# Latent attention with a linear layer, one core: PV and out-projection of the first chunk in other units, and a chunk's input loaded from ScalarE

## The reference

```python
q = (x @ wq.T).reshape(B, S, N_HEADS, QK_HEAD)          # 16 heads, 128 + 64 values
q_pe = apply_rope(q_pe, cos, sin); k_pe likewise        # the 64 rotary values
q_lat = jnp.einsum('bshd,hdc->bshc', q_nope, wkv_b_h[:, :NOPE])
kv_cache = rmsnorm(kv_lat, kv_norm_w)                   # 128 values a token, for all heads
scores = (jnp.einsum('bshc,btc->bsht', q_lat, kv_cache) + jnp.einsum('bshr,btr->bsht', q_pe, k_pe)) * SCALE
attn = jax.nn.softmax(jnp.where(causal[None, :, None, :], scores, NEG_INF), axis=-1)
out_lat = jnp.einsum('bsht,btc->bshc', attn, kv_cache)
out = jnp.einsum('bshc,hdc->bshd', out_lat, wkv_b_h[:, NOPE:])
return out.reshape(B, S, N_HEADS * VDIM) @ wo.T
```

## Time and profile before

| | us |
|---|---|
| median of three runs (lowest, highest) | 1892.62 (1886.29, 1893.92) |
| the profiled execution | 1894.48 |
| its span, first to last instruction | 1892.0 |
| lies around the span | 2.5 |
| mean granted TensorE clock | 0.969 of full speed |

### The profile page before, as it was taken

One profiled execution on the slowest core, in us unless ns is written; L12 is line 12 of the kernel. 1 busy time (PEld: TensorE's weight loads), 2 busy tenths in 40 slices (PEclk: granted clock), 3 DMA queues, 4 the chain that ended last, 5 costly groups with the idle time before them and its releaser, 6 DMA issues.

```text
span 1892.0 us, 28195 instructions
## 1 busy us (share of the span) xinstructions
PE 1717.4 (91%) x9326; PEld 1452.8 (77%) x9326; DVE 1211.1 (64%) x2801; ACT 850.7 (45%) x1358; POOL 1008.2 (53%) x635
## 2 busy tenths in 40 slices
PE   6988788878899999799999999979999999999996
PEld 5877666656778877578888888868888888888875
DVE  4674466655666677466776776657666666666663
ACT  4554334433344454345445445434544544454442
POOL 4674444442365556355655655635555565664654
PEclk9898899988999999899999999989999999999998
DMA  6995355563756656656555554555665564655543
GB/s 201 362 329 198 102 151 146 158 190 101 201 148 174 170 156 163 182 150 179 158 149 145 158 149 135 162 166 143 175 162 130 150 162 119 166 143 130 148 121 105
DMA packets 127184, 309.12 MB, mean 163 GB/s; under 512 B 29442, under 2 KB 41987, under 8 KB 125508
## 3 DMA queue, kind: packets, MB, share of 16 engines
q1 hardware_dynamic: 98720, 233.33, 43.1%
q10 hardware_dynamic: 28324, 74.05, 15.0%
HBM read 113.28 MB, written 34.60 MB: 78 GB/s over the span
## 4 chain that ended last, share of the span: by engine, by line
PE 62%; issue 11%; DVE 7%; POOL 4%; ACT 3%; DMA 1%; SPq 1%; ACTq 1%; POOLq 0%; DVEq 0%
PE p_score L1106 25%; PE p_out L1126 18%; PE p_result L1138 7%; PE p_lat L1086 7%; PE p_rot L1086 5%; POOL pT L1389 2%; DVE acc L1241 2%; DVE turned L1200 2%; ACT qp_h L1328 1%; DVE rot_sin L1216 1%; DVE probs L1178 1%; SPq L991 1%; POOL qp_l L1378 1%; POOL qp_l L1381 1%; PE p_score L1110 1%
## 5 line engine op out<-in xcount | busy, mean ns | idle before, releaser
L1389 POOL TENSOR_TENSOR pT<-pT,pT_h 128x1024 fp32r<-128x1024 f32 x320 | 688.6, 2178 | 445.5 <-ACT pT_h L1304 442.8
L1178 DVE TENSOR_SCALAR_CACHE_REDUCE probs<-p_score 128x512 f32<-128x512 f32 (+3 forms) x640 | 383.6, 602 | 433.6 <-PE p_score L1106 256.8
L1283 ACT ACTIVATE probs<-probs,neg_max 128x128 f32<-128x128 f32 (+15 forms) x256 | 307.9, 1203 | 453.8 <-DVE neg_max L1184 430.3
L1304 ACT ACTIVATE pT_h<-pT 128x1024 fp32r<-128x1024 f32 x320 | 291.1, 963 | 267.3 <-PE p_out L1126 203.6
L1200 DVE STREAM_TRANSPOSE turned<-probs 128x1024 f32<-128x1024 f32 (+7 forms) x384 | 341.8, 915 | 43.2 <-ACT probs L1283 38.5
L1126 PE MATMUL p_out<-pT_h,V_h 128*128 128x256 f32 (+3 forms) x1024 | 303.4, 296 | 18.7 <-POOL pT L1389 18.7
L1126 PE MATMUL p_out<-pT,V_h 128*128 128x256 f32 (+3 forms) x1024 | 302.7, 296 | 0.0
L1126 PE MATMUL p_out<-pT_h,V_l 128*128 128x256 f32 (+3 forms) x1024 | 302.3, 295 | 0.0
L1106 PE MATMUL p_score<-Kp,qp_h 128*128 128x512 f32 (+3 forms) x640 | 235.9, 369 | 15.6 <-POOL qp_l L1381 15.6
L1106 PE MATMUL p_score<-Kn_h,q_h 128*128 128x512 f32 (+3 forms) x640 | 240.3, 375 | 2.4 <-DVE q_l L1223 2.4
L1138 PE MATMUL p_result<-Wv,o_h 128*128 128x512 f32 x512 | 173.8, 421 | 70.9 <-DVE acc L1241 51.4
(11 more groups left out here) (135 smaller groups left out, 2384.7 us busy)
## 6 DMA issues: line engine op xcount, KB each, us to landing
pT<-turned SPq DMA_DIRECT2D x384, 128.0 KB, 3.6
Wq<-wq_scr ACTq DMA_DIRECT2D x63, 512.0 KB, 4.8
Wv<-wv_scr SPq DMA_DIRECT2D x63, 512.0 KB, 3.5
pT<-turned SPq DMA_DIRECT2D x192, 112.0 KB, 3.8
pT<-turned SPq DMA_DIRECT2D x192, 96.0 KB, 2.9
pT<-turned ACTq DMA_DIRECT2D x128, 128.0 KB, 3.9
Wp<-wp_scr SPq DMA_DIRECT2D x31, 512.0 KB, 4.4
pT<-turned SPq DMA_DIRECT2D x192, 80.0 KB, 2.6
```

Of the source, the lines that this page charges most:

```text
L1178: dve.tensor_scalar(probs[row % ROW_RING][:, b * CW:b * CW + width], p_score[n % SCORE_RING][:, 0:width], SCALE, LOWEST, ALU.mult, ALU.max ...
L1283: act.activation(probs[row % ROW_RING][:, 0:width], probs[row % ROW_RING][:, 0:width], ACT.Exp, bias=neg_max[p][:, i:i + 1], scale=1.0, ac ...
L1304: act.activation(high.rearrange("p r t i q -> p r t (i q)"), low.bitcast(F32).rearrange("p r t i q -> p r t (i q)"), ACT.Copy).then_inc(p_ ...
L1389: pool.tensor_tensor(low.rearrange("p r t i q -> p r t (i q)"), low.bitcast(F32).rearrange("p r t i q -> p r t (i q)"), high.bitcast(F32). ...
```

## The change

Seven things change, all in `build_attention` or in the functions that place work.

1. Chunk 0, PV: units 1 and 2 of slot s in place of 2 and 3. The high and low groups of slot s-2 come in unit 0 in place of 1.
2. Chunk 0, out-projection: head s-2 in unit 3, in place of head s-3 in unit 1. o_h and o_l of slot s-2 come in unit 3 of slot s, in place of unit 0 of slot s+1.
3. Chunk 1, out-projection: blocks in units 5, 6, 7, 7 in place of 6, 6, 7, 7. Slot 16 no longer does two heads.
4. Chunk 3, out-projection: units 0, 1, 2, 3 in place of 0, 1, 2, 2.
5. Rotary work: the projection in unit 0 (unit 1 in slot 15), 1, 2, 2 of the four chunks in place of 0, 0, 0, 1; the products, the sum and the splits follow. In chunks 2 and 3 the split qp_h and qp_l moves from the opening to the closing slot, unit 1.
6. xT of the next chunk is loaded by ACT behind `load_q` of the chunk's last but one head, where SP loaded it at that slot's end.
7. The rotary tables of the next chunk are loaded by SP at that slot's start.

```diff
 def value_unit(s, k):
-    return (2 + k, 1 + k, 6 - groups_of(s - 2) + k, 3 + k)[phase(s)]
+    return (1 + k, 1 + k, 6 - groups_of(s - 2) + k, 3 + k)[phase(s)]
 def high_place(s, k):
     if k < HIGH_RING:
-        return (s + 1, units_of(s + 1) - 1) if phase(s + 1) == 1 else (s + 2, 0 if phase(s + 1) == 3 else 1)
+        return (s + 1, units_of(s + 1) - 1) if phase(s + 1) == 1 else (s + 2, 1 if phase(s + 1) == 2 else 0)
 def out_heads(s):
-    if s < H:
-        return (s - 3,) if s >= 3 else ()
     if s < 2 * H:
-        return (s - 3, s - 2) if s == H else (s - 2,)
+        return (s - 2,) if s >= 2 else ()
 def out_unit(s, g, i):
-    if s < H:
-        return 1
     if s < 2 * H:
-        return 0 if g == s - 3 else 6 + i // 2
-    return 0 if s % 2 else (2 + i if phase(s) == 2 else (0, 1, 2, 2)[i])
+        return (3, (5, 6, 7, 7)[i])[phase(s)]
+    return 0 if s % 2 else i + (2 if phase(s) == 2 else 0)
+def rotary_unit(s):
+    return (1 if s == H - 1 else 0, 1, 2, 2)[phase(s)] if opens_head(s) else None
-def rotary_unit(s):
-    return 1 if phase(s) == 3 else 0
 def rotary_add_unit(s):
-    return (1, 4, 4, 5)[phase(s)] if opens_head(s) else None
+    if phase(s) == 2:
+        return 0 if not opens_head(s) else None
+    return (rotary_unit(s) + 1, 5, None, 6)[phase(s)] if opens_head(s) else None
 def rotary_high_unit(s):
-    return (2, 5, 5, 6)[phase(s)] if opens_head(s) else None
+    if phase(s) > 1:
+        return 1 if not opens_head(s) and s < SLOTS else None
+    return (rotary_unit(s) + 2, 6)[phase(s)]
...
             def slot(s):
+                if opens_head(s) and head_of(s) % H == H - 2 and chunk_of(head_of(s)) + 1 < NCH:
+                    load_tables(chunk_of(head_of(s)) + 1)
                 if 1 <= s <= SLOTS:
                     exchange(s - 1, (0, 1))
...
-                    if j + 1 < NCH and h == H - 2:
-                        load_tables(j + 1)
-                        load_chunk(j + 1)
...
+            def load_chunk(j):
+                act.wait_ge(lat_projected, H * j)
+                act.wait_ge(rot_projected, H // 2 * j)
+                act.dma_start(xT[:, :, :, :].bitcast(F32), t["xT_scr"][j]).then_inc(xT_in, 16)
...
                         if g + 2 < HEADS:
                             load_q(g + 2)
+                        if (g + 2) % H == 0 and g + 2 < HEADS:
+                            load_chunk(chunk_of(g + 2))
```

More of the change, by code:

```diff
@@ L186, in query_unit @@
     return 4 if s < SLOTS and closes_head(s) else None
+def rotary_unit(s):
+    return (1 if s == H - 1 else 0, 1, 2, 2)[phase(s)] if opens_head(s) else None
 def rotate_ops(s, u):
+    if not opens_head(s):
+        return ()
     if phase(s) == 0:
-        return range(5) if u == 0 else ()
+        return range(5) if u == rotary_unit(s) else ()
     first = rotary_unit(s) + 1
     return ((0,), (1, 2), (3, 4))[u - first] if first <= u <= first + 2 else ()
-def rotary_unit(s):
-    return 1 if phase(s) == 3 else 0
 def rotary_add_unit(s):
-    return (1, 4, 4, 5)[phase(s)] if opens_head(s) else None
+    if phase(s) == 2:
+        return 0 if not opens_head(s) else None
+    return (rotary_unit(s) + 1, 5, None, 6)[phase(s)] if opens_head(s) else None
 def rotary_high_unit(s):
-    return (2, 5, 5, 6)[phase(s)] if opens_head(s) else None
+    if phase(s) > 1:
+        return 1 if not opens_head(s) and s < SLOTS else None
+    return (rotary_unit(s) + 2, 6)[phase(s)]
 def row_unit(s, i):
@@ L1003, in load_v @@
                 sp.dma_start(Wv[:, :, :].bitcast(F32), t["wv_scr"][g % H]).then_inc(wv_in, 16)
-            def load_chunk(j):
-                sp.wait_ge(lat_projected, H * j)
-                sp.dma_start(xT[:, :, :, :].bitcast(F32), t["xT_scr"][j]).then_inc(xT_in, 16)
             def load_tables(j):
@@ L1143, in slot @@
                 for u in range(units_of(s)):
-                    rotary = u == rotary_unit(s) and opens_head(s) and g % 2 and g + 1 < HEADS
+                    rotary = u == rotary_unit(s) and g % 2 and g + 1 < HEADS
                     if rotary and s < H:
@@ L1256, in slot @@
                             split_output(old)
-                    if opens_head(s) and g % 2 and g + 1 < HEADS:
+                    if g % 2 and g + 1 < HEADS:
                         for op in rotate_ops(s, u):
@@ L1356, in _ @@
                 act.wait_ge(stored["wq"][i], 16 * H // 2)
+            act.wait_ge(stored["xT"], 16 * (NCH - 1))
             load_q(1)
```

## The result

The changed kernel takes 1969.31 us (1967.98 to 1973.28, four runs) where the kernel before takes 1893.1 (1886.29 to 1893.92, four runs): 4.0% slower, the ratio between 1.0377 and 1.0424 at 95%. Forecast were 1969, within 1936 to 2014, and slower with a chance of 0.92. The profiled execution has a span of 1966.5 us for 1892.0, at a mean granted clock of 0.959 for 0.969.

What follows compares the result with a forecast made beforehand. PE, busy for 91% of the span, was taken as the bound. Terms of 78 (chunk 0) - 8 - 9 + 12 + 3 made +76 on the profiled 1894.5, 1970, so 1969 us by the runs' median, range 1936 to 2014.

Steps and rivals of the forecast that it cites:

- slots 3 to 15: Chunk 0: a loop through Wv's wait and quarter 2 closes once a slot; thirteen periods of 22.3 us for 219.4, +70.5.
- chunk 1, slots 17 to 30: Chunk 1: first out-projection block waits about 0.9 us for o_l, low groups pushed 0.5 in even slots; +3, bounds -12 and +15.
- hole at chunk 2 (slot 31): PE's wait for xT at chunk 2: an earlier load leaves 3 us of 11.25 and removes most half clock; -8.
- hole at chunk 3 (slots 62, 63): PE's wait for xT at chunk 3: an earlier load leaves 2 us of 9.32; -9 with the clock.
- chunk 3 (slots 64 to 94): Chunk 3: qp_l between POOL's groups makes PE wait 0.9 us in 15 closing slots, +14; fewer p_result waits, -2.
- The steps of the loop: Chunk 0, from out-projection end E: quarter 2 E + 5.3, first PV E + 9.0, o_l E + 16.6, next E at E + 19.9.
- the same in odd and even slots: Sign in slots 4 to 15: time between equal instructions is 20 to 25 us, equal in odd and even slots.
- The clock's share: Chunk 0's loop: half speed after each hole adds 2.4 us a period, giving 22.3; bounds nothing and 8.3.
- the slack of 1.8 us: Chunk 3: PE takes POOL's fourth group 1.8 us after it ends; 2.7 of qp_l then leaves a wait of 0.9.
- The low clock through chunk 0: Rival, chance 0.09: all loop PE work in chunk 0 at half speed, a period of 28.2 us, total 2046.
- The looser loop: Rival, chance 0.07: chunk 0's exchange lands in time and only the wait for o_l is new; total 1899.
- Faster: Rival, chance 0.04: chunk 0's PV and out-projection find inputs ready, slots take 13.5 us, 175.5 for 219.4; total 1834.

Runs made afterwards that it cites:

- e3: The kernel before with only chunk 0's edits (PV, groups, out-projection moved): 1973.7 us, ratio 1.0405.
- e1: The changed kernel with SP issuing quarter 2 of the exchange ahead of the load of Wv in chunk 0 too: 1889.45 us, ratio 0.9965.
- e8: The changed kernel with SP's order kept but a second Wv buffer in chunk 0, so Wv waits for the out-projection one head further back: 1897.56 us, ratio 1.003.
- e9: The kernel before with quarter 2 of the exchange issued ahead of Wv in chunk 0: 1897.38 us, ratio 1.0008.
- e10: e7 with the load of the rotary weights Wp behind quarter 2 of the exchange in chunk 0: 1847.42 us, ratio 0.9748.
- e2: The kernel before with xT loaded by ACT behind Wq and the tables at the slot's start: 1881.11 us, ratio 0.9917.
- e6: The changed kernel with chunk 3's split qp_h and qp_l in unit 4 of the closing slot in place of unit 1: 1939.35 us, ratio 1.0243.
- e4: The changed kernel with chunk 3's rotary work back in its old units: 1941.04 us, ratio 1.0254.
- e7: The changed kernel with e1's and e4's edits; in chunk 0 also o_l ahead of DVE's unit 3 score copy, qp_h behind o_h: 1857.25 us, ratio 0.9807.

## Why the prediction was right

The table compares slots' lengths of the two traces, in us, with the terms of the forecast.

| term | forecast | measured |
|---|---|---|
| chunk 0, slots 0 to 2 | +5 | +6.0 |
| slots 3 to 15 | +70.5 | +58.7 |
| slot 16 | +3 | +1.6 |
| chunk 1, slots 17 to 30 | +3 | +1.1 |
| hole at chunk 2 (slot 31) | -8 | -11.5 |
| slots 32 to 61 | 0 | +3.1 |
| hole at chunk 3 (slots 62, 63) | -9 | -10.6 |
| chunk 3 (slots 64 to 94) | +12 | +27.2 |
| sum | +76 | +75.6 |

The mechanism and its place were right: e3 has the whole slowdown with chunk 0 alone, e1 takes it away and e8 most of it through SP's order and wait alone, e9 shows that the order was harmless before. The sum is better than its terms, of which two were off by 12 and 15 us and cancelled; that it meets the total within 1 us is luck.

**The steps of the loop.** From the end E of the out-projection, in the 13 turns: Wv issued at E + 0.03, as before; quarter 2 landed at E + 4.8 to 5.4 in 12 of 13 turns and once at 6.4 (forecast 5.3); first PV at E + 8.5 to 9.0 and once 10.1 (9.0); out-projection at E + 17.3 to 19.1 (16.6, and 2.4 for the clock). The waits for POOL are 6.0 in even slots and 3.2 in odd ones (6 and 3), those for o_l 1.6 (1.8 by its steps, from E + 14.8 to E + 16.6). The mean turn is 21.55 for the 22.3 forecast. The turns don't quite agree: nine take 20.8 to 21.5 us and four 22.3 to 22.6. And "the same in odd and even slots" holds from one Wv issue to the next: cut at DVE's first copy, most slots alternate between 24 and 19 us, since 2.8 us of rotary projection lie on one side of it.

**The clock's share.** It was the open term, with 2.4 a turn, between 0 and 8.3. The 854 PE instructions of slots 3 to 15 are busy for 194.8 us in the changed kernel and for 169.96 in e10, at a clock of 0.99: 24.8 / 13 = 1.9 us a turn. The windows of the clock agree: in the 13 turns it stood at 0.50 in 12 stretches, eight of 6.8 us and four of 3.4, with 52.0 us of PE work in them. Half of that is 26.0, for 12.9 in five stretches before and 1.5 in one of e10. It is the half speed around the end of the hole, as forecast, though not in every turn: the last, with a hole of 3.3 us, has none. Around the hole that ends at 392.10:

```profile
391.20:398.00 6.80, 5.91 (x16) 4.98 (x17) 0.72 (x3) 1.29 (x4) 1.98 (x2) 0.50 0.16 38
```

0.50 is 1.2 GHz, the lower of the two levels. The clock fell 5.1 us into the hole of 5.96, 0.9 us ahead of PE's first matmul. The Trainium skill ("TensorE: Matmul & The Clock Gate", section "HAM oscillation — how this bites in real kernels") describes a loop that starts every pass cold behind a wait for DMA. This trace agrees for 12 of 13 turns, with its 24.8 us; the sum without that term would have been 1938. The rest of the difference to the forecast turn, 0.25 us or so, is spread over the steps.

**The part of slots 3 to 15 that was too high.** 22.3 for 21.55 is 9.8 us in 13 turns. The window by DVE's copies is 2 us shorter than 13 turns, since its two ends lie on different sides of a rotary projection.

**The load of xT.** Both holes nearly closed, from 11.25 and 9.32 to:

```profile
839.23 3.01 PE L1082 MATMUL p_rot<-xT,Wp 128*128 128x512 f32 x12 [1.22 <-issue]
...
1296.19 3.00 PE L1082 MATMUL p_rot<-xT,Wp 128*128 128x512 f32 x12 [1.46 <-issue]
```

and the three loads of xT took this long from issue to landing:

```profile
DMA to landing us min/median/max: 8.2/8.5/10.5
```

I had 3 and 2 us left; xT landed in 8.5 at the median, not 10.9, and nothing of the half clock stayed in slot 31. The Trainium skill ("DMA: Bandwidth & Descriptors", section "Issuing engines are not separate DMA queues") says that another issuing engine saves the sequencer's time alone, which it calls usually small. No run here shows more bandwidth by it: in the kernel before the loads landed in 9.5 to 11.6 us from SP, and in e2, the same kernel but for the load, in 8.1 to 12.5 from ACT. But what e2 saved, 15 us in three loads, is the time that SP's queue held the load behind its own waits, and that isn't small.

**Chunk 3: the step that was mis-sized.** The mechanism was named, the two qp_l between POOL's third and fourth group. The timeline answers to the earlier trace rows:

```profile
1458.10 7.16 POOL L1394 TENSOR_TENSOR pT<-pT,pT_h 128x1024 fp32r<-128x1024 f32 x3 [4.83 <-ACT pT_h L1300]
...
1465.38 1.28 POOL L1383 TENSOR_TENSOR qp_l<-rotated,qp_h 64x512 fp32r<-64x512 f32 x1
...
1466.74 1.28 POOL L1386 TENSOR_TENSOR qp_l<-rotated,qp_h 64x512 fp32r<-64x512 f32 x1
...
1468.17 2.35 POOL L1394 TENSOR_TENSOR pT<-pT,pT_h 128x1024 fp32r<-128x1024 f32 x1
...
1470.57 0.38 PE L1122 MATMUL p_out<-pT_h,V_h 128*128 128x256 f32 x1 [1.89 <-POOL pT L1394]
```

PE waits 1.9 us here, not 0.9. This is the closing slot of an odd head; in those of even heads it waits 1.1, and together 21.0 for the 14 forecast. Three parts of the term were mis-sized.

The first is the slack of 1.8 us. In the kernel before it held for both kinds of closing slot. This is one of an odd head:

```profile
1404.99 9.50 POOL L1389 TENSOR_TENSOR pT<-pT,pT_h 128x1024 fp32r<-128x1024 f32 x4 [2.59 <-ACT pT_h L1304]
...
1416.24 0.28 PE L1126 MATMUL p_out<-pT_h,V_h 128*128 128x256 f32 x1
```

The groups end at 1414.49, and PE takes the fourth 1.75 later. But the change itself takes 0.8 of it away in the closing slots of odd heads. In e6, where nothing stands between the groups, they end at 1461.67 and PE comes 0.9 later (the rows above); in e4, with the rotary work in its old units, it comes 1.7 later again. So it is the moved rotary work that used up the slack; which of its steps wasn't tried apart. The second part is what stands between the groups: from the end of the third, 1465.26, to the start of the fourth, 1468.17, it is 2.9 us, not 2.7. Less 0.9 or 1.75 of slack, that makes the two waits.

The third part I had left out: the clock. At six places of chunk 3 it stood at half for 3.4 us, once behind a wait of 2.9 us and five times in the closing slots with 1.9, and PE's instructions take 10.2 us more (556.00 for 545.76), 1.7 for each place. This part is not fixed by the program. In e1 and e8 chunk 3 is the same and PE waits the same 21.0 us for POOL, yet the clock fell in two of the seven closing slots with 1.9 only, and chunk 3 took 582.7 and 583.0 us in place of 588.5. One of the places in the changed kernel:

```profile
1394.70:1398.10 3.40, 3.40 (x12) 2.59 (x12) 0.16 (x1) 0.38 (x1) 0.00 (x0) 0.50 0.48 187
```

The waits of p_result behind `accumulate` are 7.4 for 10.9, -3.5 where I had -2.

**The rivals.** The low clock through chunk 0 would have shown 28.2 a turn: 21.55. The looser loop needed ACT's high groups not to wait for quarter 2: they waited 13 times. Faster needed Wv's wait to end 4 to 6 us earlier. That condition was right as far as it went: with the wait gone (e1) chunk 0 falls to 208.1, below the 219.4 of before, and with DVE's, ACT's and SP's orders put right to 193.8 (e10), a turn of 14.9. The 175.5 that I gave for it isn't reached: PE is still idle for 23.8 us there, of which 16.3 are the wait for o_l, 1.25 a slot.

What stays open: why the clock falls behind a wait of 1.9 us in one closing slot and not in another, in five of seven in one execution and in two of seven in two others; and which step of the moved rotary work took the 0.8 us of slack.

## What to carry to other kernels

A DMA queue is a program with waits in it. Whoever moves an engine's work within a period has to ask which queue entry waits for that work and what is queued behind the entry: here a load with a single buffer, harmless in the middle of a slot, closed a loop over four engines once its wait ended at the slot's end, and swapping two lines was worth 80 us. Slack read in the kernel before need not be there after the change: here the same edit that put 2.9 us of work into it had moved other work too, and half of the slots lost 0.8 us of it. A short wait is priced with the stretch at half clock that may follow it, as a range, since the same wait had it in some slots and executions only. When one wait of a loop goes, look at once for the one that was hidden behind it: it took back 9 of some 14 us in e7.

## What the runs showed of the hardware

- The clock fell to 0.50 for a stretch of 3.4 us, from 1394.7 for one, behind a wait of only 1.9 us in a closing slot of chunk 3: in five of seven such slots of the changed kernel, in two of seven in e1 and in e8. Such a fall costs 1.7 us, nearly as much as the wait.
- A 64 KB DMA of the exchange lands in about 2.0 us with no other load ahead of it or beside it (e10), in the slots shown in 3.4 to 4.1 with a load of 512 KB issued beside it (e10), in 5.0 to 5.3 with a second one issued ahead of it (e7), and in 5.5 to 6.1 with three (e8).
